# Sorted MoE on one core: scatters of rows that wait for the scatter two places in front

## What is computed

```python
    def _L1_ffn_ref(x, gate_w, bias, up_w, up_b, down_w, down_b, sw_up, sb_up, sw_down, sb_down):
        ...
        xf = x.reshape(-1, h)
        scores = jax.nn.sigmoid(xf @ gate_w + bias)
        top_scores, top_idx = jax.lax.top_k(scores, K)
        top_scores = top_scores / (jnp.sum(top_scores, axis=-1, keepdims=True) + 1e-06)
        w = jnp.zeros((T, E), dtype=xf.dtype).at[jnp.arange(T)[:, None], top_idx].add(top_scores)
        up = jnp.einsum('th,ehi->tei', xf, up_w) + up_b
        hact = jax.nn.gelu(up, approximate=False)
        eo = jnp.einsum('tei,eih->teh', hact, down_w) + down_b
        combined = jnp.einsum('teh,te->th', eo * 0.1, w)
        shared = (jax.nn.gelu(xf @ sw_up + sb_up, approximate=False) @ sw_down + sb_down) * 0.1
        out = (shared + combined).reshape(b, s, h)
        return out / (jnp.max(jnp.abs(out), axis=-1, keepdims=True) + 1e-06)
    ...
    x = x + 0.5 * _L1_ffn_ref(_layernorm(x, axis=-1), ...)
    x = x + _L1_attn_ref(_layernorm(x, axis=-1), ...)
    x = x + 0.5 * _L1_ffn_ref(_layernorm(x, axis=-1), ...)
```

## Time and profile before

| | |
|---|---|
| three runs | 1555.86, 1561.59, 1562.26 us; median 1561.59 |
| the profiled execution | 1572.32 us, its span from first to last instruction 1570.2 us |
| TensorE busy | 1286.0 us, 82% of the span |
| VectorE, ScalarE, GpSimd busy | 964.0, 827.2 and 676.2 us (61, 53 and 43%) |
| scatters, L1483 | 128 indirect DMAs, 126.2 us of GpSimd |
| stores of results, L1489 | 156 indirect DMAs, 152.5 us of GpSimd |
| DMA | 164.76 MB, mean 105 GB/s |

### The profile page before, as it was taken

The page is one execution under the profiler, slowest core; times in us unless marked ns, Lnnn a source line. Parts: engine busy times, 40 slices in busy tenths (PEclk is TensorE's granted clock), DMA queues, the critical chain, the costliest instruction groups (busy, mean ns, idle before and its releaser), DMA issues. The chain is left out here.

```text
span 1570.2 us, 30207 instructions
## 1 busy us (share of the span) xinstructions
PE 1286.0 (82%) x8434; PEld 725.2 (46%) x8434; DVE 964.0 (61%) x2082; ACT 827.2 (53%) x1988; POOL 676.2 (43%) x880
## 2 busy tenths in 40 slices
PE   2987999999999698884789974988998796568993
PEld 1761222222222376553689861221222254568983
DVE  5787898898898186500223744899989740023455
ACT  0221788888888434421356653666665451235661
POOL 3123223223220222474445531788788537354442
PEclk9995999999999799786899996899998888689996
DMA  5970222212220100212457742444444121346774
GB/s 116 170 155 1 72 73 82 71 43 69 71 72 22 19 16 2 59 49 83 126 159 209 223 120 77 150 155 140 150 141 147 64 71 60 97 127 177 221 212 129
DMA packets 161935, 164.76 MB, mean 105 GB/s; under 512 B 31389, under 2 KB 113771, under 8 KB 161800
## 3 DMA queue, kind: packets, MB, share of 16 engines
q1 hardware_dynamic: 150592, 145.92, 34.2%
q0 software_dynamic: 9088, 16.94, 3.1%
q10 hardware_dynamic: 2120, 0.28, 0.1%
HBM read 115.45 MB, written 45.90 MB: 103 GB/s over the span
## 5 line engine op out<-in xcount | busy, mean ns | idle before, releaser
L1193 DVE TENSOR_REDUCE at_nm<-at_mx 128x2 f32<-128x1024 f32 x256 | 303.9, 1220 | 40.5 <-PE at_mx L1036 39.2
L1139 ACT ACTIVATE at_probs<-at_ring 128x512 f32<-128x512 f32 x512 | 269.4, 605 | 47.4 <-PE at_ring L1048 45.8
L1539 ACT ACTIVATE m_hidden<-m_pU,mw_up_b 128x128 f32<-128x128 f32 x624 | 178.7, 371 | 127.7 <-PE m_pU L1745 70.6
L1489 POOL DMA_INDIRECT pair_rows<-m_y,m_y_id x156 | 152.5, 977 | 203.0 <-DVE m_y L1686 123.3
L1754 PE MATMUL m_pD<-m_down_all,m_hidden 128*128 x1248 | 175.9, 286 | 37.5 <-ACT m_hidden L1539 30.9
L2236 POOL TENSOR_TENSOR ss_hc<-ss_h,ss_c_all 128x512 f32<-128x512 f32 x128 | 161.7, 1270 | 52.3 <-DVE ss_h L2406 45.5
L1745 PE MATMUL m_pU<-m_hidden,m_up_now 128*128 128x128 f32 x1248 | 174.4, 285 | 7.3 <-issue 6.5
L1754 PEld LDWEIGHTS m_pD<-m_down_all,m_hidden 128*128 128x128 f32 x1248 | 158.9, 199 | 43.7 <-issue 42.9
L1048 PE MATMUL at_ring<-at_qq,at_kk 51*128 51x512 bf16 x512 | 163.3, 386 | 7.1 <-ACT at_probs L1139 6.1
L1036 PE MATMUL at_mx<-at_kk,at_qq 48*128 48x512 bf16 x512 | 156.0, 399 | 13.1 <-DVE at_nm L1193 8.0
L1745 PEld LDWEIGHTS m_pU<-m_hidden,m_up_now 128*128 128x128 f32 x1248 | 160.6, 201 | 9.6 <-issue 9.6
(11 more groups left out here) (319 smaller groups left out, 1948.7 us busy)
## 6 DMA issues: line engine op xcount, KB each, us to landing
m_up_now<-in_L_ffn_up_w_dram SPq DMA_DIRECT2D x156, 256.0 KB
ss_dtb<-ss_dt_rows SPq DMA_DIRECT2D x128, 256.0 KB
sorted_rows<-empty_row SPq DMA_DIRECT2D x2, 5070.0 KB, 47.2
m_xb<-sorted_rows SPq DMA_DIRECT2D x156, 65.0 KB
m_hidden<-pair_rows SPq DMA_DIRECT2D x32, 256.0 KB
at_qq<-q_stack SPq DMA_DIRECT2D x64, 96.0 KB, 2.2
at_kk<-k_stack SPq DMA_DIRECT2D x64, 96.0 KB, 2.3
m_down_all<-in_L_ffn_down_w_dram SPq DMA_DIRECT2D x16, 256.0 KB, 4.3
```

Of the source, the lines that this page charges most:

```text
L1139: act.activation(probs[:, (slot % 2) * GH + ORDER[j], :], ring[bank][:, :], ACT.Exp, scale=SCALE).then_inc(s.exp_done, 1)
L1193: dve.tensor_reduce(nm[group % 2][:, 2 * (pair % 2) + parity, 2 * half:2 * half + 2], mx[parity][:, :, :], AX.X, ALU.max, negate=True).the ...
L1489: pool.indirect_dma_start(pair_rows, bass.IndirectOffsetOnAxis(ap=y_id[j % Y_BUFS][:, :], axis=0), y[j % Y_BUFS][:, :], None, bounds_check ...
L1539: act.activation(hid[j % T_BUFS][:, k, :], pU[j % 2][:, k * P:(k + 1) * P], ACT.Gelu, bias=v.up_b[:, bass.ds(e, 1), k:k + 1].rearrange("p ...
```

## The change

Two semaphores, `scattered[0]` and `scattered[1]`, take turns over all 64 scatters of one MoE, in the order n in which GpSimd issues them. Before scatter n (n of 2 and more) GpSimd waits until the one with number n - 2 has landed, so that at most two are under way. The waits of GpSimd before the marks (0,1) and (1,1), and those of SyncE before each half, now ask both semaphores for the number of scatters up to there.

```diff
--- before.py
+++ after.py
@@ -1239,6 +1239,7 @@
 PAIR_ROWS = 2 * NB * L
 HB = (2 * HT * P + E1 * (P - 1)) // P
 TB = HALVES * HB
+SCATTERS = 2
 X_BUFS, Y_BUFS, T_BUFS, U_BUFS = 8, 12, 3, 6
 FINISH_AT, PIECES = 8, 5
 Y_LOAD_AT = {11: (0, 1), 18: (2,), 23: (3,)}
@@ -1355,7 +1356,7 @@
     s = m.s
     sorted_rows, pair_rows = dram
     xT_all, logit, gate_b = m.xT_all, m.logit, m.gate_b
-    scattered = [[sem(f"{tag}_scattered{h}{k}") for k in range(2)] for h in range(HALVES)]
+    scattered = [sem(f"{tag}_scattered{i}") for i in range(SCATTERS)]
     xb_in = [sem(f"{tag}_xb_in{i}") for i in range(X_BUFS)]
     y_out = [sem(f"{tag}_y_out{i}") for i in range(Y_BUFS)]
     y_in = [sem(f"{tag}_y_in{i}") for i in range(2)]
@@ -1437,8 +1438,8 @@
                              ).then_inc(s.experts_in, 16)
             sp.wait_ge(s.list_ready, 1)
             for half in range(HALVES):
-                for k in range(2):
-                    sp.wait_ge(scattered[half][k], 16 * HT)
+                for i in range(SCATTERS):
+                    sp.wait_ge(scattered[i], 16 * (2 * HT * (half + 1) // SCATTERS))
                 for j in range(HB):
                     load_block(half * HB + j)
                     load_up(half * HB + j)
@@ -1478,11 +1479,18 @@
                 pool.tensor_copy(v.rows[:, tiles, ID:ROW], v.idw[:, k, tiles, :]).then_inc(s.marked, 1)
                 pool.wait_ge(s.marked, 2 * half + k + 1)
 
+            def wait_scattered(n):
+
+                for i in range(SCATTERS):
+                    pool.wait_ge(scattered[i], 16 * (n // SCATTERS))
+
             def scatter(half, k, t):
-                at_tile = half * HT + t
+                at_tile, n = half * HT + t, (2 * half + k) * HT + t
+                if n >= SCATTERS:
+                    pool.wait_ge(scattered[n % SCATTERS], 16 * (n // SCATTERS))
                 pool.indirect_dma_start(sorted_rows, bass.IndirectOffsetOnAxis(ap=index[:, k, at_tile:at_tile + 1], axis=0),
                                         v.rows[:, at_tile, :], None, bounds_check=TB * P - 1, oob_is_err=False
-                                        ).then_inc(scattered[half][k], 16)
+                                        ).then_inc(scattered[n % SCATTERS], 16)
 
             def put(j):
                 pool.wait_ge(s.y_ready, j + 1)
@@ -1495,14 +1503,14 @@
             pool.wait_ge(s.placed, 1)
             for t in range(HT):
                 scatter(0, 0, t)
-            pool.wait_ge(scattered[0][0], 16 * HT)
+            wait_scattered(HT)
             mark(0, 1)
             for t in range(HT):
                 scatter(0, 1, t)
             mark(1, 0)
             for t in range(HT):
                 scatter(1, 0, t)
-            pool.wait_ge(scattered[1][0], 16 * HT)
+            wait_scattered(3 * HT)
             mark(1, 1)
             for j in range(HB):
                 if j < HT:
```

## The result

The changed kernel takes 1568.22 us (median of 8 runs, 1560.87 to 1570.62), the kernel before 1557.82 us beside it (8 runs, 1554.47 to 1563.46). The ratio of the means is 1.0056, 95% interval [1.0033, 1.0079]: slower by half a per cent, just over what a measurement of this kernel can tell from no change, where 1540 us had been predicted.

A forecast was written before the change was run, and what follows sets the result against it. TensorE was taken to bound the kernel, starved while GpSimd issues scatters back to back. Two MoEs at 10.8 us each take 21.6 us from 1572.32, giving 1550.7, or 1540 as a median; range 1512 to 1592.

The forecast's parts named there:

- (a): Semaphores of the scatters: two in place of four, with the same increments, cost 0.
- (b): Waits in the first three scatter lists: 0.64 us per pair, 4.5 us a list, 13.4 us in one MoE.
- (c): Shared expert beside the lists: GpSimd's pauses let TensorE run at 0.83 of full rate, ending near 1326.
- The coefficient of 4.2: Full-rate work of the other engines, in us, bought by each us of GpSimd idle time beyond 0.31 us.
- (d): Alternating scatters and stores: 8 blocks ready at store 0, store 16 at 1409.0 against 1419.83, gain 10.8 us a MoE.
- rival B: Lasting relief: the alternating stretch is GpSimd's alone, store 16 at 1403.5, total 1487 us; chance 0.11.
- So the gain stays: Behind store 16 TensorE bounds the loop before and after, busy 0.96 of the time, keeping the 10.8 us.
- The base: Whole kernel: profiled execution 10.7 us above the median before; the same difference taken from 1550.7 gives 1540.0.
- A: Three lists: the 0.9 us pause relieves nothing, all moves by 13.4 us twice, 1588.4 us; chance 0.28.
- C: Whole kernel: nothing moves, waits never felt or price and relief cancel, 1561.6 plus or minus 7; chance 0.11.

The follow-up runs named there:

- d1c: The changed kernel with SyncE's first load held until three lists have landed; 1577.92 us, 1.0066 of the kernel before.
- l1c: The kernel before with a wait for the scatter two places in front in the first two lists alone; 1556.61 us, 0.9919 of the kernel before.
- m1: The kernel before with a 0.56 us GpSimd memset ahead of every second scatter of the first three lists, no added waits; 1543.02 us, 0.9893 of the kernel before.
- groups 1 and 4: Two sets of follow-up runs on the same chip, each beside the unchanged kernel before, which took 1559.99 and 1571.42 us.
- traces from B: Profiles from the second kind of chip (three chips), among them the unchanged kernel before, 1457.39 us in its one run there.
- on A: Runs on the one chip of the first kind, where the unchanged kernel before took 1559.99 and 1571.42 us.

## Why the prediction was wrong, point by point

**One slip of counting.** The store at 1419.83 is the 16th, 15 intervals behind store 0 (3.46 us each), not "store 16" after 16. The sum should have had 15 x 2.55 = 38.3 us instead of 40.8, and 3.46 - 2.55 = 0.91 for a pause instead of 0.69, a gain of 11.5 us instead of 10.8; it does not change the sign. Smaller: the 2.37 us of idle GpSimd at 1301.8 include the copy's 0.21; without them the first estimate is 8.8 / (2.16 - 0.31) = 4.8 us per us instead of 4.3.

**(a) Semaphores, 0.** Nothing in the runs speaks against it; it was not tried by itself.

**(b) The price of a pair. This step failed.** Right for the first two lists: list (0,1) starts at 28.0 and 27.8 us instead of 23.6 and 23.5, the forecast 4.5 us a list; SyncE's first load came 8.9 us later (45.1 to 54.0), as forecast. Wrong for the third: it was priced with a landing of 2.42 us. Scatter (1,1,0) moved by 24.6 us (67.2 to 91.8), not 13.4. Landings of 4 us make a pair about 4.8 us; 7 x (4.8 - 3.19) = 11.3 us is that difference. d1c shows that SyncE's loads, or the work that they release, make it: 26.7 and 27.3 us for the list with the loads held, 38 with them. l1c shows what it is worth: 12.4 us of the median come back when the waits leave that list. The relief itself brought the loads at their full pace into the list: in those 23 us the DMA share was 0.32 while TensorE starved, and is 0.56 now that it takes up blocks. The bounds of this term were landings of 2.28 us, from a quiet stretch, and 2.54 us, from beside SyncE's loads while TensorE starved; none was from beside loads at their full pace. The waits sum to 50.4 us, not 27.

**(c) The relief.** Right in kind, too small in size: full rate instead of 0.83, the shared expert's end 42.2 us from the first scatter, not 45.3 (1326 on the clock of before, whose first scatter is at 1280.74). The coefficient of 4.2 is too low: for m1's gap of 0.71 us it gives 4.2 x 0.40 / 2.95 = 0.57 of full rate, and m1 has 1.0. TensorE's loop starts 55.8 us from the first scatter; the forecast was 57.3 (near 1338).

**(d) The value of the blocks in hand. This step failed too.** At store 0 TensorE has begun the down products of 14 blocks (8 were forecast to be ready; with 14, all 12 buffers of results are taken), so GpSimd makes no pause in the stretch, as rival B said: 38.3 us for 15 intervals instead of 51.9. Late as store 0 is (93.1 us, not 82.0), the 16th store comes 7.0 and 7.7 us earlier than before, not far from the 10.8 that were forecast. But that store does not measure what TensorE has done. The pauses that GpSimd had spent waiting for a starved block were also what let the others run, by my own coefficient; I took them out of GpSimd's time and charged nobody. In the first MoE after has 14 blocks at 91 us, 17 at 104, and no further one until 135; before has 14 at 128.5. The lead, 10 blocks at 94.5 us (14 against 4), is 3 at 128.5 us, worth 3 x 1.9 = 5.7 us, and behind the stretch GpSimd waits 5.72 us for a block. "So the gain stays" was wrong for that reason: 7.0 and 7.7 us at the 16th store are 4.5 and 6.0 at the 40th and 2.3 and 5.1 at the end of the loop. This is read from one trace of before and two of the changed kernel, which have the same 14 and 17 blocks; no run takes this step by itself.

**The base.** I took the difference of 10.7 us between the profiled execution of before and its median as a constant. The profiled pair moved by -11.4 us, half of the forecast; the medians by +10.4. Since executions differ mostly in the two loops, a run of 1560 us has presumably starved less than the traced one, and had less to win. Which stretch was shorter in it is open: no trace of before near 1560 us is there. So the traces alone show a change that gains less than forecast; that it loses by the medians is shown by the runs and, for the third list, by l1c, but its sum isn't closed term by term. The same kernel took 1559.99 us and 1571.42 in groups 1 and 4, so its time is not fixed even on one chip.

**The rivals.** A (no relief) fell: the shared expert ends at 42 us. B was half right: GpSimd never pauses, but the stops come back. C's "price and relief cancel" describes the sum best, with another price and another relief than it named. The Trainium skill (Runtime: NRT & Kernel Launch, Instruction fetch mechanics) has it that what it costs to fetch the next block of instructions is mostly hidden. The traces from B agree (37.09 of 38.80 us busy beside 31 indirect DMAs); on A (9.10 of 39.80) something isn't hidden. That it is instruction fetch was not shown.

## What to carry over

A wait on a landing is a pause whose length depends on what else the DMA engines do (27 us for a list with the loads held, 38 beside them): price it with the landing in the stretch where it will be met after the change, not in the quiet one of before. Where only the pause is wanted, a short memset gives it at a fixed price (0.9893 against 1.0055 in one group on A). And if idle time of one engine is what keeps the others running, removing it in a later stretch has to be charged to them there. Before keeping such a change, time it on more than one chip and beside runs of the kernel before taken at the same time, since the three edits that gained on A and ran on B lost there (1.010 to 1.019).

## What the runs showed of the hardware

- One program took 1558 to 1571 us (medians) on A, and 1458 to 1460 on the three chips of B; 114.5 of the 114.9 us between two traces lie between the first scatters and the ends of the two loops.
- On A, indirect DMAs of GpSimd with 0.30 us between them can all but stop TensorE, ScalarE and VectorE (11 matmuls in 23 us in the earlier trace rows; 16.55 and 17.23 us without one). It does not set in at once: the first list of 16 left TensorE at full rate (20.60 of 20.60 us). 0.71 us in every second gap freed the shared expert (end at 42 us), 0.39 us little of it (75.6 and 55.1 us).
- A scatter of 128 rows lands in 2.28 us in a quiet stretch (DMA share 0.15), in 2.54 beside loads while TensorE starves (DMA share 0.32) and, by the waits, in about 4.0 beside loads at a DMA share of 0.56.
